# Graph attention over gathered edge rows, 25 target nodes at a time with four heads stacked, in place of counted edges and dense attention

## The reference

```python
q = (x @ Wq + bq).reshape(n, H, OUT_DIM)      # n = 1250, H = 4, OUT_DIM = 512
k = (x @ Wk + bk).reshape(n, H, OUT_DIM)
v = (x @ Wv + bv).reshape(n, H, OUT_DIM)
alpha = jnp.einsum('ehc,ehc->eh', q[dst], k[src]) / np.sqrt(OUT_DIM)
amax = jax.ops.segment_max(alpha, dst, num_segments=n)
ex = jnp.exp(alpha - amax[dst])
denom = jax.ops.segment_sum(ex, dst, num_segments=n)
attn = ex / denom[dst]
msg = attn[:, :, None] * v[src]
agg = jax.ops.segment_sum(msg, dst, num_segments=n).reshape(n, HC)
x_attn = agg + x @ Wskip + bskip
x_lin = x_attn @ Wlin + blin
h = x_lin + x_attn[:, :OUT_DIM]               # then a layernorm with gamma, beta, added to x
...
summed = jax.ops.segment_sum(edge_attr, col, num_segments=x.shape[0])
count = jax.ops.segment_sum(jnp.ones((edge_attr.shape[0],), dtype=x.dtype), col, num_segments=x.shape[0])
agg = summed / jnp.maximum(count, 1.0)[:, None]
```

## Time and profile before

| | |
|---|---|
| runs, us | 2218.78 to 2223.68, median 2220.4 |
| span of the profiled execution, us | 2220.5 |
| instructions | 36706 |
| moved by DMA | 156.34 MB |

### The profile page before, as it was taken

The page is one execution under the profiler, slowest core; times in us unless marked ns, Lnnn a source line. Parts: engine busy times, 40 slices in busy tenths (PEclk is TensorE's granted clock), DMA queues, the critical chain, the costliest instruction groups (busy, mean ns, idle before and its releaser), DMA issues. The chain is left out here.

```text
span 2220.5 us, 36706 instructions
## 1 busy us (share of the span) xinstructions
PE 2059.9 (93%) x13310; PEld 1806.2 (81%) x13310; DVE 1323.4 (60%) x2952; ACT 836.3 (38%) x1586; POOL 360.1 (16%) x308
## 2 busy tenths in 40 slices
PE   7998998999999999999999689999998999999586
PEld 5776667899999999999988569989878888888475
DVE  4574784443453454453678645556557878878766
ACT  3663993221221122122221312333336555555421
POOL 1000111000000000000000101111314453554243
PEclk9998999999999999999999889999998999999798
DMA  8760003122121211130101220201421021120542
GB/s 263 225 192 2 23 23 94 50 75 64 37 84 36 64 66 55 41 83 18 48 34 37 97 86 1 96 19 38 151 72 27 20 56 28 28 56 9 170 151 97
DMA packets 79516, 156.34 MB, mean 70 GB/s; under 512 B 7429, under 2 KB 22338, under 8 KB 77854
## 3 DMA queue, kind: packets, MB, share of 16 engines
q1 hardware_dynamic: 69802, 134.63, 20.1%
q0 software_dynamic: 4960, 11.49, 1.6%
q10 hardware_dynamic: 4616, 8.40, 1.1%
HBM read 104.17 MB, written 50.32 MB: 70 GB/s over the span
## 5 line engine op out<-in xcount | busy, mean ns | idle before, releaser
L130 PE MATMUL psum<-pt_hi,xn_hi 125*128 125x250 f32 x800 | 225.0, 281 | 3.3 <-DVE yt_lo L1188 1.6
L131 PE MATMUL psum<-pt_lo,xn_hi 125*128 125x250 f32 x800 | 223.8, 280 | 0.0
L132 PE MATMUL psum<-pt_hi,xn_lo 125*128 125x250 f32 x800 | 222.8, 278 | 0.0
L2412 POOL TENSOR_TENSOR mprob<-mprob,mrden 125x1250 f32<-125x1250 f32 x80 | 181.7, 2272 | 229.9 <-DVE mrden L2518 229.4
L1122 ACT ACTIVATE prob<-prob,nb 125x1250 f32<-125x1250 f32 x40 | 53.7, 1342 | 346.0 <-DVE nb L1215 346.0
L131 PE MATMUL psum<-xt_lo,t_hi 128*125 128x512 f32 (+1 forms) x480 | 170.1, 354 | 0.0
L132 PE MATMUL psum<-xt_hi,t_lo 128*125 128x512 f32 (+1 forms) x480 | 169.8, 354 | 0.0
L130 PE MATMUL psum<-xt_hi,t_hi 128*125 128x512 f32 (+1 forms) x480 | 169.1, 352 | 0.0
L2441 ACT ACTIVATE mprob<-psum,mbias 125x1250 f32<-125x1250 f32 x80 | 104.3, 1304 | 157.7 <-DVE mbias L2527 157.7
L130 PEld LDWEIGHTS psum<-pt_hi,xn_hi 125*128 125x128 f32 x800 | 151.2, 189 | 3.9 <-DVE yt_lo L1188 2.0
L2525 DVE TENSOR_REDUCE mmin<-psum 125x1 f32<-125x512 f32 (+1 forms) x240 | 127.1, 584 | 44.4 <-PE psum L2684 44.1
(11 more groups left out here) (503 smaller groups left out, 5854.7 us busy)
## 6 DMA issues: line engine op xcount, KB each, us to landing
slots_in<-slots_blank SPq DMA_DIRECT2D x12, 1282.5 KB, 9.2
cnt<-edge_counts SPq DMA_DIRECT2D x40, 305.2 KB
q_chunk<-q_store SPq DMA_DIRECT2D x40, 250.0 KB, 6.1
edge_attr<-in_attr SPq DMA_DIRECT2D x4, 1204.0 KB
slots_in<-slots_blank SPq DMA_DIRECT2D x3, 1539.0 KB, 16.0
moe_xg<-slots_in SPq DMA_DIRECT2D x17, 256.5 KB
raw_WvT<-in_WvT SPq DMA_DIRECT2D x4, 1024.0 KB, 6.0
raw_WskipT<-in_WskipT SPq DMA_DIRECT2D x4, 1024.0 KB, 11.8
```

What stands on the lines that cost most here:

```text
L130: nc.tensor.matmul(out, lh, rh, start=start, stop=False)
L131: nc.tensor.matmul(out, lh, rl, start=False, stop=False)
L132: return nc.tensor.matmul(out, ll, rh, start=False, stop=stop)
L2412: nc.gpsimd.tensor_tensor(prob[:, n % 4, :], prob[:, n % 4, :], rden[:, n % 4:n % 4 + 1].broadcast_to([P, N]), ALU.mult).then_inc(p_ready, 1)
```

## The change

`count_edges` is gone, and with it the counts, their loads and the split of the edge attributes in `prepare`. In place of it `prepare` finds for each of 50 windows of 25 target nodes where its edges begin in the sorted list, in steps of ten edges, and how many passes over at most 500 edges the longest window needs; each engine reads that number and repeats the whole loop so often. The layernorm of x is stored to DRAM (`xn_store`).

`graph_attention` makes the skip products as before, but stores them to DRAM (`base_store`), then T for all four heads one after the other (80 units of 12 matmuls of 250 columns), stored to `t_store`. Then comes a loop over the 50 windows. For a window SP loads 500 edge indices (`edges_in`, four ahead) and attributes (`attr_load`, one ahead), POOL gathers 500 rows of `xn_store` by source in four indirect transfers (`gather`, three ahead), PE turns them (`turn_rows`), multiplies them with the window's T of all four heads stacked in 100 rows (`scores`), adds a large negative number for edges of other targets (`mask`), sums attributes (`edge_sums`), turns the probabilities (`turn_prob`), sums the gathered rows with them (`values`) and turns the result (`turn_values`). After five windows one tile of 125 targets goes through the output products of all heads (`outputs`, 48 matmuls of 512 columns). The splits are divided among ACT (tops), DVE (rests) and POOL (`rest`, two of four slots). In the loop SP also writes blank rows to `slots_in` (`blanks`), two tiles of 128 rows in each window up to the 40th and one in the 41st, from a DRAM tensor `blank_rows`. `acc` is loaded from `base_store` at the loop's start, and each pair of tiles is stored back when its outputs are added. `finish` runs three steps for each pair of tiles but the last in later windows.

The core of the diff:

```diff
-GROUP = 4
-GROUPS = -(-EDGES // (GROUP * P))
-ET = GROUPS * GROUP
 EDGE_D = 64
-PARTS = 3 * EDGE_D + 2
+HEADS = 4
+WIN = 25
+WINDOWS = N // WIN
+SLOTS_E = 4
+RANGE = SLOTS_E * P
+HW = HEADS * WIN
+BLOCK_E = 10
+BLOCKS = EDGES // P // BLOCK_E
+ROUNDS = -(-EDGES // RANGE)
+PER_TILE = P // WIN
+ATTR = 2 * EDGE_D + 2
...
+            for t in range(NT):
+                sp.wait_ge(skip_added, t + 1)
+                sp.dma_start(g.base_store[t * P:(t + 1) * P, :], skip_out[:, t % 4, :]).then_inc(skip_stored[t % 4], 16)
...
+            def attr_load(t, first):
+                if t:
+                    sp.wait_ge(attr_low, t)
+                sp.dma_start(attr[:], w["attr"][bass.ds(first, RANGE), :].rearrange("(p s) c -> p s c", s=SLOTS_E)
+                             ).then_inc(attr_in, 16)
...
-            def blank_slots(first, n):
-                dst = g.slots_in[bass.ds(128 * first, 128 * n), :].rearrange("(i p) d -> p i d", p=128)
-                sp.dma_start(dst, bc(blank[:], n)).then_inc(blank_out, 16)
...
+            def blanks(first, n):
+                dst = g.slots_in[128 * first:128 * (first + n), :].rearrange("(i p) d -> i p d", p=128)
+                src = g.blank.rearrange("(i p) d -> i p d", i=1).broadcast_to([n, 128, D + 1])
+                sp.dma_start(dst, src).then_inc(blank_out, 16)
...
+            with sp.Fori(0, passes) as turn:
+                firsts = [edges_in(t) for t in range(4)]
+                attr_load(0, firsts[0])
+                t_load(0, 0), t_load(0, 1)
+                for m in range(KT):
+                    sp.wait_ge(t_stored[m], 16 * HEADS * NC)
+                for c in range(NC):
+                    sp.dma_start(g.acc[:, 2 * c:2 * c + 2, :], pair(g.base_store, c)).then_inc(base_in, 16)
+                for t in range(WINDOWS):
+                    r, pos = divmod(t, PER_TILE)
+                    if t + 4 < WINDOWS:
+                        sp.wait_ge(hot_done, t + 1)
+                        sp.wait_ge(xe_ready, t + 1)
+                        firsts.append(edges_in(t + 4))
+                    if t + 1 < WINDOWS:
+                        attr_load(t + 1, firsts[t + 1])
+                    if pos == 2 and r + 1 < NT:
+                        sp.wait_ge(t_low, t + 1)
+                        t_load(r + 1, 0)
+                    if pos == 4 and r + 1 < NT:
+                        sp.wait_ge(t_low, t + 1)
+                        t_load(r + 1, 1)
+                    if t < 41:
+                        blanks(2 * t, 2 if t < 40 else 1)
+                    c, step = divmod(t, 2 * PER_TILE)
+                    if step == 6 and c < FIN:
+                        if c:
+                            sp.wait_ge(xin_used, 2 * c)
+                        sp.dma_start(fin.xin[:], pair(w["x"], c)).then_inc(xin_in, 16)
+                    if step == 3 and c:
+                        sp.wait_ge(o_added, 2 * c)
+                        sp.dma_start(pair(g.base_store, c - 1), g.acc[:, 2 * c - 2:2 * c, :]).then_inc(base_out, 16)
...
+            def gather(t):
+                pool.wait_ge(index_in[t % 4], 16 * (t // 4) + 16)
+                if t >= 4:
+                    pool.wait_ge(y_done, t - 3)
+                for s in range(SLOTS_E):
+                    nc.gpsimd.indirect_dma_start(xe[t % 4][:, s, :], None, g.xn_store,
+                                                 bass.IndirectOffsetOnAxis(ap=index[t % 4][:, s, 0:1], axis=0)
+                                                 ).then_inc(xe_in[t % 4], 16)
...
+            def rest(t):
+                pool.wait_ge(xe_top, 2 * t + 2)
+                pool.wait_ge(x_done, KT * t + KT)
+                for s in (2, 3):
+                    last = nc.gpsimd.tensor_tensor(xe_lo[t % 4][:, s, :], xe[t % 4][:, s, :], f32(xe_hi[t % 2][:, s, :]),
+                                                   ALU.subtract)
+                last.then_inc(xe_pool, 1)
...
+                for t in range(WINDOWS):
+                    rest(t)
+                    if t + 1 < WINDOWS:
+                        offsets(t + 1)
+                        others(t + 1)
+                    if t + 2 < WINDOWS:
+                        landed(t + 2, turn)
+                    if t + 3 < WINDOWS:
+                        gather(t + 3)
...
+                for t in range(WINDOWS + 1):
+                    now, more = t < WINDOWS, t + 1 < WINDOWS
+                    if more:
+                        for k in range(KT):
+                            x_hi(t + 1, k)
+                        t_tops(t + 1)
+                    if now:
+                        exponentials(t)
+                    if more:
+                        attr_hi(t + 1)
+                    if t:
+                        y_rows(t - 1)
+                    if now:
+                        p_hi(t)
+                    if more:
+                        rows_hi(t + 1, 0)
+                    if t:
+                        yt_tops(t - 1)
+                    if more:
+                        rows_hi(t + 1, 1)
...
+                for t in range(WINDOWS + 1):
+                    now, more = t < WINDOWS, t + 1 < WINDOWS
+                    if more:
+                        for k in range(KT - 1):
+                            x_lo(t + 1, k)
+                    if now:
+                        maxima(t)
+                    if more:
+                        x_lo(t + 1, KT - 1)
+                        t_lows(t + 1)
+                        hots(t + 1)
+                    if now:
+                        sums(t)
+                    if more:
+                        attr_lo(t + 1)
+                    if now:
+                        p_lo(t)
+                    if more:
+                        rows_lo(t + 1)
+                    if t:
+                        yt_lows(t - 1)
+                    if t >= PER_TILE and t % PER_TILE == 0:
+                        edge_sums(t // PER_TILE - 1)
+                    if t > PER_TILE and t % PER_TILE == 1:
+                        add_out((t - 1) // PER_TILE - 1)
+                    for c in range(FIN):
+                        finish(c, t - 2 * PER_TILE * c)
...
+            for h in range(HEADS):
+                pe.wait_ge(m_low, KT * h + KT)
+                for c in range(NC):
+                    for m in range(KT):
+                        u = KT * (NC * h + c) + m
+                        if u >= 2:
+                            pe.wait_ge(t_copied, u - 1)
+                        for k in range(KT):
+                            last = three_pass(nc, unit_bank(u), [a[h % 2][:, k, m * 128:(m + 1) * 128] for a in (m_hi, m_lo)],
+                                              [a[:, k, c * CH:(c + 1) * CH] for a in (g.xt_hi, g.xt_lo)], k == 0, k == KT - 1)
+                        last.then_inc(u_done, 1)
...
+            def scores(t, k):
+                pe.wait_ge(x_low, KT * t + k + 1)
+                three_pass(nc, score, [a[:, k, :] for a in (t_hi, t_lo)], [a[:, k, :] for a in (xt_hi, xt_lo)],
+                           k == 0, k == KT - 1).then_inc(s_done, 1)
...
+                for t in range(WINDOWS + 1):
+                    now, more = t < WINDOWS, t + 1 < WINDOWS
+                    if now:
+                        pe.wait_ge(t_low, t + 1)
+                        if t:
+                            pe.wait_ge(e_done, 2 * t - 1)
+                        for k in range(KT):
+                            scores(t, k)
+                            if k == 0:
+                                mask(t)
+                            if more:
+                                turn_rows(t + 1, k)
+                        edge_sums(t)
+                    if t > PER_TILE and t % PER_TILE == 1:
+                        outputs((t - 1) // PER_TILE - 1)
+                    if t:
+                        values(t - 1)
+                    if now:
+                        turn_prob(t)
+                    if t:
+                        turn_values(t - 1)
+                outputs(NT - 1)
...
         prepare(core, g, w, ln)
-        count_edges(core, g)
         graph_attention(core, g, w)
```

1136 lines of the change are left out of this document (531 added, 605 removed).

## The result

| | before | after |
|---|---|---|
| runs, us | 2218.78 to 2223.68 | 2270.7 to 2281.38 |
| median, us | 2221.1 (2220.4 in the three runs above) | 2274.7 |
| ratio, 95% interval | | 1.024 (1.0219 to 1.026) |
| span of the profiled execution, us | 2220.5 | 2279.3 |

A forecast was written before the change was run, and what follows sets the result against it. PE's work bounds the kernel before; in the new loop, blanks on two DMA engines would. 371 + 701 + 109 + 24 + 11 = 1216, plus 992.7 behind, gives 2209 us; 8 in 10 between 2040 and 2275.

The forecast's parts named there:

- signs of being wrong: `prepare` ending outside 200 to 205, first window not past by 375, windows without blanks under 12.5 or over 15 us.
- about 2 us of waits: Skip products before T: waits on copies of their first factor, added to 28 us of matmuls, ending at 235.5.
- the hand-made chain of 13.65: Loop window across engines: 10.3 us laid out by hand, 2.2 for outputs, about 1.0 for DVE delays; PE's work 11.0.
- the 992.7 taken as fixed: Stages behind the last addition into `acc` at 1227.8: left alone by the change, so 992.7 us as before.
- stall on the second window's attributes: Loop start: five loads of `acc` ahead of the attributes take 20 us, stalling about 16; steady loop from 371.
- 41 windows at the transfers' pace: Loop windows with blanks: two DMA engines carry the blanks and set 17.1 us a window, 701 us; chance 0.60.
- The blanks' term: Blanks' share of a loop window: 263 KB on each of two engines at 23.1 GB/s, 11.4 us.
- 8 windows without blanks: Last loop windows, after the blanks are written: run at the chain's 13.65 us each, 109 us.
- The granted clock: PE's clock in the loop: may fall to 0.83, hidden behind transfers; in the first rival up to 2 us a window.
- the first (the chain sets the pace): Rival for the loop: transfers don't hold it up, 13.65 us in every window, 2068 us; chance 0.32.
- Port contention: Second rival, loop: DVE and POOL hold each other up at SBUF, 20.05 us a window, 2381 us; chance 0.08.
- break-even of 16.8 us a window: Loop pace at which the change neither gains nor loses: (1227.8 - 371 - 35) / 49.

The follow-up runs named there:

- c3_spread: Changed kernel with blanks over all engines, skip-row stores ahead of the constants' loads, and output matmuls spread between score steps: 2166.8 us, 0.9744 of the kernel before.
- c1_wide_rest: Changed kernel with blanks over all engines and POOL's two subtractions waiting for the window's maximum: 2198.2 us, 0.9885 of the kernel before.
- e3_rest: Changed kernel, blanks still narrow, with POOL's two subtractions waiting for DVE's window maximum: 2272.7 us, 1.0232 of the kernel before.
- f5_loop: Changed kernel with large-piece blanks in the loop, new front, spread outputs, later acc loads, masks before POOL's subtractions, sixteen DVE writes: 2086.9 us, 0.9401 of the kernel before.

## Why the prediction was wrong

It forecast 2209 us and faster; measured were 2274.7 and slower. Three of its own signs of being wrong came out: `prepare` ended at 191.3 (200 to 205 were given), the first window's exponentials stood at 389.6 (by 375), and the windows without blanks took 16.5 us (12.5 to 15). What failed is the path: the terms "about 2 us of waits" before T, the hand-made chain of 13.65, and the 992.7 taken as fixed. Against the profiled execution 2279.3 - 2208.7 = 70.6 us are missing:

- **The front, +18.4 to the first T product.** The first skip product came 12.5 us earlier than assumed (I had counted the edge splits that leave `prepare` at nothing, within 5 us). The skip products then took 61 us and not 30. This is the step "about 2 us of waits on the copies". I asked which DMAs are issued, and not what SP's queue holds ahead of the store that frees a buffer: 20 loads of the constants, four matrices and four rows stood there.
- **T, +7.3.** 80 units at 1.404 are 112.3; the starts of its copies are 118.2 us apart over 79, with a few waits for stores and matrices.
- **The first window, +8.4,** and its stall. The first exponentials came 15.9 us behind the last T unit, where the first scores were forecast 7.5 behind it; why isn't shown. The stall on the second window's attributes was forecast at 16 and is there at 22.64:

```profile
389.57 0.28 ACT L1135 ACTIVATE corr<-max_table,max_scaled 100x1 f32<-100x1 f32 x1
412.50 0.42 ACT L1128 ACTIVATE edge_attr_hl<-edge_attr 125x256 fp32r<-125x256 f32 x1 [22.64 <-DMA edge_attr<-in_attr]
```

  Counted back one pace from the second window's `corr` (421.22 - 17.07), the steady loop starts at 404 and not 371: the 34 us of these three points, less 1, as the stall with its surroundings adds 14.5 us to the interval and not 16.
- **41 windows at the transfers' pace, -1.** Forecast 17.1, measured 17.07 (in four other kernels with narrow blanks 17.13 to 17.32). The blanks on two engines do hold the loop up: wide ones take 1.8 us a window away, double ones add 8.0. But that the transfers alone set the pace is wrong, and the number came out by luck. The blanks' term was 11.4 us and the trace's pieces give 10.1. With doubled blanks 25.09 - 19.7 = 5.4 us are left for the rest, if the two engines never rest there (an estimate), where the forecast had 5.7. Together 15.5, about what the first ten intervals take (15.34). The other thirty take 17.65, since waits of the chain, which the prediction let hide behind the transfers, come on top of them; with wide blanks the same thirty take 16.04, and not 13.65.
- **8 windows without blanks, +23.** 16.5 and not 13.65. With wide blanks the same eight take 16.5 too, so the hand-made chain was too short and not the blanks' after-effect. Runs name two parts of it. The outputs stand whole in it, as assumed, but spreading them takes 14.5 us off the eight (`c3_spread`); the wait of the maximum at the port takes 5.3 (`c1_wide_rest`). A third part is read from the intervals alone: the three windows with steps of `finish` take some 8 us more than their neighbours (19.8 and 29.7 beside 11.5 to 14.3 with wide blanks), where the forecast had about 1.0 a window for it with the additions and edge sums. The granted clock is a rival that no run separates: it was 0.87 in these eight windows (1104 to 1236 us) and 0.89 to 0.95 with wide blanks, the chain was summed at full pace, and the prediction had put 0.83 at up to 2 us a window. It had named 12.5 to 15 us as the bounds of the chain; this is over them.
- **The stages behind, +16.5.** "In stages that the change leaves alone" was true of the code and not of its time: self-attention took 443.4 us and not 426.9, and sixteen DVE instructions ahead of it take 22 us off it.
- **The tail, -1.** From the last exponentials to the next stage's first instruction 36.7 us forecast (35, and the 1.7 taken off the stages behind), 35.6 measured.

Of the rivals, the first (the chain sets the pace) is out: with the blanks spread the loop is 1.8 us a window faster, so they did hold it up; and its 13.65 would have been 1.6 too short even then (15.25). Port contention was priced on the wrong side: I let POOL's small instructions wait, and it was DVE's that waited, 2144 ns for one column. L2006, DVE's with both inputs in SBUF, had shown that direction: its 40 took 419 to 2627 ns, median 421, mean 892. Taking its wait away changed nothing with narrow blanks (`e3_rest`) and 9 us with wide ones. The break-even of 16.8 us a window held only for a start at 371 and 992.7 us behind the loop; with the 404 and the 16.5 us that were measured it is (1227.8 - 404 - 35 - 16.5) / 49 = 15.8. The changed kernel's 49 windows took 17.0 each, those with wide blanks 15.4, and so one is slower than the kernel before and the other a little faster.

The rule that I took from the Trainium skill, "DMA: Bandwidth & Descriptors", the paragraph on how many engines, fits these runs: with the outermost dimension 2 the blanks' pieces run two at a time and the loop loses what it doesn't lose with 128 or 16; with 16 up to 16 run at once.

Still open: what makes the chain's waits and the transfers add up to 17.65 where neither alone is over 16.04, why the first scores came late, what part the clock has, and what beyond the port, `finish` and the outputs holds a window of 11.5 us above the 10.3 laid out by hand.

## What to carry to other kernels

Read the outermost dimension of every transfer, and what stands ahead of it in its queue: a write that nobody waits for held a loop up, and a store behind 20 small and 8 larger loads stopped PE for 20 us. When a change replaces long runs of matmuls by many short windows with a static order, price the chain over the engines, not the busiest engine: PE lost 201 us of work and the kernel took 54 us more. Before a difference of 1% is given to an edit, look whether the stages that it doesn't touch took the same time. And a forecast that hits the mean of a loop is no proof of what limits it: look at its parts, here the first ten windows and the rest.

## What was not expected of the hardware

- DRAM to DRAM over all engines in rows of 2052 bytes, beside the stores of T, ran at 149 to 164 GB/s with the engines full, where blanks from SBUF ran at 334 to 370; a row took 0.212 us in the mean there and 0.105 in the loop. Pieces of 43,776 bytes, two at a time, took 1.68 us, 26 GB/s each, more than the 23 of an engine in the blanks from SBUF.
- A one-column DVE instruction with two tables in SBUF as inputs takes 2.86 us while two POOL subtractions run one behind the other, and ends with the second; free of them it takes 0.22 us in the mean (`f5_loop`).
- The same 80 softmax steps took 421.1, 426.9, 442.1 or 443.4 us; in each of the two kernels only the sixteen DVE writes ahead of them were added.
